# A two-layer convolution on one Trainium2 core: parameters loaded first, a shorter chain for the generated kernels, new queue orders for quads 2 and 3, new banks for the last pairs, one image normalised on GpSimd

## What is computed

```
x: (16, 32, 48, 48) float32
# L0: a (32, 32, 9, 9) kernel is generated from (sx, sy, angle) per channel pair
a = c*c*sx2 + s*s*sy2 ; b = c*s*(sx2 - sy2) ; d = s*s*sx2 + c*c*sy2 ; det = a*d - b*b
q = ia*xx*xx + 2*ib*xx*yy + id*yy*yy ; ker = exp(-0.5*q) ; ker /= sum(ker)
x = x + conv9x9(groupnorm(x, 16 groups), ker, zero padding) + bias
# L1: 5x5, reflect padding
x = x + conv5x5(groupnorm(x, 16 groups), weight)
```

## Time and profile before

| what | value |
|---|---|
| median of 3 runs | 280.61 us (280.49 to 281.2) |
| the profiled execution's own time | 280.59 us |
| its span, first to last instruction | 278.6 us |
| mean granted TensorE clock | 0.962 |
| busy PE | 228.2 us (82%) |
| busy DVE | 222.1 us (80%) |
| busy ACT | 156.9 us (56%) |
| busy POOL | 3.4 us (1%) |

### The profile page before, as it was taken

How to read it: one execution, slowest core, us unless ns; L and a number is a source line. 1 busy time by engine, 2 the same in 40 slices (tenths; PEclk the granted TensorE clock), 3 DMA queues, 4 the chain that set the end, 5 groups by cost and what they waited for, 6 DMA issues and landing times.

```text
span 278.6 us, 4041 instructions
## 1 busy us (share of the span) xinstructions
PE 228.2 (82%) x1388; PEld 138.3 (50%) x1388; DVE 222.1 (80%) x483; ACT 156.9 (56%) x320; POOL 3.4 (1%) x12
## 2 busy tenths in 40 slices
PE   0043766999799999997989999329999999996995
PEld 0042433566466566554646565115666665652552
DVE  1989999968999999999984999995168078987533
ACT  2966357998869757996629184407257002574310
POOL 1300000000000000000000000000000000000000
PEclk9998699999999999999999999859999999997999
DMA  7940001322004200035020000035200001522022
GB/s 256 358 178 0 0 0 46 85 65 65 0 0 118 69 0 2 1 90 177 5 85 2 0 0 4 1 104 166 87 0 0 2 0 30 154 88 85 2 85 85
DMA packets 7780, 17.37 MB, mean 62 GB/s; under 512 B 3280, under 2 KB 3920, under 8 KB 7760
## 3 DMA queue, kind: packets, MB, share of 16 engines
q1 hardware_dynamic: 6944, 16.78, 18.4%
q10 hardware_dynamic: 816, 0.33, 0.4%
HBM read 5.51 MB, written 4.72 MB: 37 GB/s over the span
## 4 chain that ended last, share of the span: by engine, by line
DVE 49%; PE 29%; ACT 10%; issue 9%; DMA 2%; DVEq 0%; ACTq 0%
PE banks L1253 17%; PE banks L1238 12%; DVE X L687 8%; DVE lo L654 6%; ACT P L974 3%; ACT junk L956 3%; DMA prm<-in_w 2%; DVE X L706 2%; DVE s L619 1%; DVE wl L513 1%; DVE arg L501 1%; DVE partU L609 1%; DVE partU L602 1%; ACT hi L997 1%; DVE wl L539 1%
## 5 line engine op out<-in xcount | busy, mean ns | idle before, releaser
L1238 PE MATMUL banks<-hi,wh 128*128 128x368 f16 (+4 forms) x288 | 51.8, 326 | 15.0 <-ACT wh L1029 6.2
L1238 PE MATMUL banks<-lo,wh 128*128 128x368 f16 (+4 forms) x288 | 50.4, 320 | 0.0
L1238 PE MATMUL banks<-hi,wl 128*128 128x368 f16 (+4 forms) x288 | 50.3, 320 | 0.0
L1238 PEld LDWEIGHTS banks<-hi,wh 128*128 128x128 f16 x288 | 27.9, 100 | 33.9 <-issue 10.9
L956 ACT ACTIVATE junk<-X 128x576 bf16<-128x576 f32 x60 | 41.0, 684 | 2.5 <-DVE X L687 0.5
L1253 PE MATMUL banks<-lo,wh 128*128 128x384 f16 x160 | 33.2, 340 | 8.4 <-DVE lo L654 8.4
L1238 PEld LDWEIGHTS banks<-lo,wh 128*128 128x128 f16 x288 | 28.2, 98 | 17.2 <-issue 0.2
L1238 PEld LDWEIGHTS banks<-hi,wl 128*128 128x128 f16 x288 | 28.1, 98 | 17.0
L1253 PE MATMUL banks<-hi,wh 128*128 128x384 f16 x160 | 32.1, 332 | 4.3 <-DVE X L712 2.8
L1253 PE MATMUL banks<-hi,wl 128*128 128x384 f16 x160 | 32.7, 336 | 0.0
L997 ACT CAST hi<-work 128x416 f16<-128x416 f32 x32 | 16.5, 539 | 20.8 <-DVE work L661 12.8
(11 more groups left out here) (127 smaller groups left out, 240.2 us busy)
## 6 DMA issues: line engine op xcount, KB each, us to landing
X<-in_x SPq DMA_DIRECT2D x8, 576.0 KB, 9.9
out<-X SPq DMA_DIRECT2D x7, 576.0 KB, 2.9
work<-X SPq DMA_DIRECT2D x8, 432.0 KB, 3.8
work<-X SPq DMA_DIRECT2D x8, 144.0 KB, 3.6
wh<-work SPq DMA_DIRECT2D x12, 72.0 KB, 2.1
wl<-work SPq DMA_DIRECT2D x12, 72.0 KB, 2.0
stage<-in_w SPq DMA_DIRECT2D x1, 640.0 KB, 7.1
work<-X SPq DMA_DIRECT2D x32, 12.0 KB, 2.3
```

The source lines that it names most:

```text
L1238: ins = nc.tensor.matmul(dst[:, :, o0:o1], wbuf[1][:, i, t * P:(t + 1) * P], src[:, :, o0 + dx:o1 + dx], start=(part == 0 and at == 0), st ...
```

## The change

- SyncE issues `prm` as its first load; the bias goes from SyncE to ScalarE, behind the tables.
- `covariance` and `exponent_parts` do several small products in one instruction each (`q` is numbered anew, and the squares 1, 4, 9, 16 come from the tables). GpSimd's two operations go to VectorE. The offsets are made by `offsets(1, 1)` and, behind the exponents of group 1, `offsets(2, 4)`. The exponentials wait for both, since they write over `centre`.
- The kernel sum takes one reduction over all taps (the outer taps counted twice) in place of one for each group.
- GpSimd normalises image 3 of quad 0; ScalarE the other three.
- `step(2)` and `step(3)` become `third_quad` and `fourth_quad`, with other orders on VectorE and ScalarE; `small_stats(1, 3)` and its square root stand earlier in the second quad. TensorE's order and SyncE's other orders stay.
- Pairs 6 and 7 get other banks than pairs 4 and 5.

```diff
-BANKS2 = ((6, 2, 3, 0), (1, 4, 5, 6))
+BANKS2 = ((6, 2, 3, 0), (1, 4, 5, 6)) * 3 + ((2, 3, 0, 1), (4, 5, 6, 2))
...
+            sp.dma_start(prm[:, :, :], w0).then_inc(prm_loaded, 16)
             load(0)
             load(1)
             sp.dma_start(stage[:, :, :], w1).then_inc(stage_loaded, 16)
-            sp.dma_start(bias_c[1][:, :], bias).then_inc(bias_loaded, 16)
...
             def covariance():
                 mul = ALU.mult
-                done(tt(wq[:, 0, :], prm[:, :, 0], prm[:, :, 0], mul))
-                done(tt(wq[:, 1, :], prm[:, :, 1], prm[:, :, 1], mul))
+                done(tt(wq[:, :, :], prm[:, :, 0:2].rearrange("p o a -> p a o"), prm[:, :, 0:2].rearrange("p o a -> p a o"), mul))
+                stage_end()
+                done(tt(q[:, 5, :], wq[:, 0, :], wq[:, 1, :], ALU.subtract))
...
                 stage_end()
-                done(tt(q[:, 1, :], scq[:, 1, :], wq[:, 0, :], mul))
-                done(tt(q[:, 2, :], scq[:, 0, :], wq[:, 1, :], mul))
-                done(tt(q[:, 3, :], scq[:, 0, :], wq[:, 0, :], mul))
-                done(tt(q[:, 4, :], scq[:, 1, :], wq[:, 1, :], mul))
-                done(tt(q[:, 5, :], wq[:, 0, :], wq[:, 1, :], ALU.subtract))
-                stage_end()
-                done(tt(q[:, 6, :], q[:, 1, :], q[:, 2, :], ALU.add))
-                done(tt(q[:, 7, :], q[:, 3, :], q[:, 4, :], ALU.add))
+                done(tt(q[:, 1:5, :].rearrange("p (a b) o -> p a b o", a=2), wq[:, :, :].unsqueeze(2).to_broadcast([P, 2, 2, C]),
+                        scq[:, :, :].unsqueeze(1).to_broadcast([P, 2, 2, C]), mul))
                 done(tt(q[:, 8, :], q[:, 0, :], q[:, 5, :], mul))
                 stage_end()
+                done(tt(q[:, 6:8, :], q[:, 2:0:-1, :], q[:, 3:5, :], ALU.add))
+                done(tt(q[:, 10, :], q[:, 8, :], q[:, 8, :], mul))
+                stage_end()
                 done(tt(q[:, 9, :], q[:, 6, :], q[:, 7, :], mul))
-                done(tt(q[:, 10, :], q[:, 8, :], q[:, 8, :], mul))
                 stage_end()
                 done(tt(q[:, 11, :], q[:, 9, :], q[:, 10, :], ALU.subtract))
                 stage_end()
                 done(nc.vector.reciprocal(q[:, 12, :], q[:, 11, :]))
                 stage_end()
-                done(stt(q[:, 13, :], q[:, 7, :], -0.5, q[:, 12, :], mul, mul))
-                done(tt(q[:, 14, :], q[:, 8, :], q[:, 12, :], mul))
-                done(stt(q[:, 15, :], q[:, 6, :], -0.5, q[:, 12, :], mul, mul))
-                stage_end()
-                MARK["quadratic"] = count[0]
+                done(stt(q[:, 13:15, :], q[:, 6:8, :], -0.5, q[:, 12, :].unsqueeze(1).to_broadcast([P, 2, C]), mul, mul))
+                done(tt(q[:, 15, :], q[:, 8, :], q[:, 12, :], mul))
+                stage_end()
...
                 dve.wait_ge(tab_loaded, 16)
-                done(tt(centre, per_row(yy2_t), per_chan(q[:, 15, :]), mul))
-                for k in range(1, 5):
-                    done(ts(ak[:, k - 1, :], q[:, 13, :], float(k * k), None, mul))
+                done(tt(centre, per_row(yy2_t), per_chan(q[:, 13, :]), mul))
+                done(tt(ak[:, :, :], squares_t.unsqueeze(2).to_broadcast([P, PAD1, C]),
+                        q[:, 14, :].unsqueeze(1).to_broadcast([P, PAD1, C]), mul))
                 stage_end()
                 done(tt(centre, centre, per_row(mask_t), ALU.add))
-                stage_end()
-                MARK["centre"] = count[0]
-                for k in (3, 2, 1):
-                    done(tt(ca_rows(k), centre, per_chan(ak[:, k - 1, :]), ALU.add))
-                    MARK["offset", k] = count[0]
+                done(tt(bt[:, :, :], per_row(yy_t), per_chan(q[:, 15, :]), mul))
+                stage_end()
+            def offsets(first, last):
+                n = last - first + 1
+                at = slice(first - 1, last)
+                done(tt(ca[:, at, :].rearrange("p k (e o) -> p k e o", o=C), centre.unsqueeze(1).to_broadcast([P, n, NE, C]),
+                        ak[:, at, :].unsqueeze(2).to_broadcast([P, n, NE, C]), ALU.add))
+                MARK["offsets"] = count[0]
+                stage_end()
             def exponents(g):
                 btf = bt[:, :, :].rearrange("p e o -> p (e o)")
                 for t in range(3 * g, 3 * g + 3):
                     k = t - PAD1
                     if k != 0:
-                        if abs(k) == PAD1:
-                            dve.wait_ge(exponents_pool, 2)
-                        else:
-                            dve.wait_ge(exponents_pool, 1)
-                            dve.wait_ge(dve_w, MARK["offset", abs(k)])
                         done(stt(arg[:, t, :], btf, float(k), ca[:, abs(k) - 1, :], ALU.mult, ALU.add))
                 MARK["exponents", g] = count[0]
...
                 done(tt(slot(1)[:, at, :], slot(2)[:, at, :], block1(1)[:, at, :], ALU.add))
                 MARK["blocks", g] = count[0]
-            def tap_sums(g):
-                dve.wait_ge(dve_w, MARK["blocks", g])
-                at = slice(3 * g, 3 * g + 3)
-                done(nc.vector.tensor_reduce(ksg[:, g, :], slot(1)[:, at, :].rearrange("p k (r o) -> p o (k r)", o=C), AX_X, ALU.add))
             def kernel_sum():
-                stage_end()
-                done(stt(ksum[:, :], ksg[:, 0, :], 2.0, ksg[:, 1, :], ALU.mult, ALU.add))
+                dve.wait_ge(dve_w, MARK["blocks", 0])
+                done(stt(twice, slot(1)[:, 0:3, :], 2.0, slot(1)[:, 3:6, :], ALU.mult, ALU.add))
+                stage_end()
+                done(nc.vector.tensor_reduce(ksum[:, :], twice.rearrange("p k (r o) -> p o (k r)", o=C), AX_X, ALU.add))
                 MARK["ksum"] = count[0]
             def kernel_reciprocal():
...
                 angles()
                 covariance()
                 exponent_parts()
+                offsets(1, 1)
                 exponents(1)
+                offsets(2, PAD1)
                 exponents(0)
                 first_stats()
                 exponents(2)
                 for at, g in enumerate((1, 0)):
                     block_sums(g, at)
-                    tap_sums(g)
                 kernel_sum()
                 outer_sum1(0)
...
-                ends1(2)
-                stream1(2, 0)
-                stream1(2, 7)
+                streams1_ends(2)
                 low_halves(1, 2, range(2, 4))
                 middle2(1)
                 rows2(1)
-                wide1(2)
-                for i in (3, 4, 5, 6):
-                    stream1(2, i)
+                small_stats(1, 3)
+                streams1_wide(2)
                 low_halves(1, 2, range(4, 8))
                 end2(1, 2)
                 end2(1, 3)
...
+            def third_quad():
+                small_stats(2, 1)
+                middle1(2, 0)
+                rows1(2, 0)
+                end1(2, 2)
+                end1(2, 3)
+                streams2(2)
+                low_halves(2, 2, range(4))
+                middle1(2, 1)
+                rows1(2, 1)
+                streams1_near(3)
+                low_halves(1, 3, range(2))
+                streams2(3)
+                middle1(2, 2)
+                rows1(2, 2)
+                low_halves(2, 3, range(2))
+                middle2(2)
+                rows2(2)
+                low_halves(2, 3, range(2, 4))
+                end2(2, 2)
+                end2(2, 3)
+            def fourth_quad():
+                streams1_ends(3)
+                low_halves(1, 3, range(2, 4))
+                middle2(3)
+                rows2(3)
+                streams1_wide(3)
+                low_halves(1, 3, range(4, 8))
+                end2(3, 2)
+                end2(3, 3)
+                small_stats(2, 2)
+                middle1(3, 0)
+                rows1(3, 0)
+                streams2(4)
+                low_halves(2, 4, range(4))
+                end1(3, 2)
+                end1(3, 3)
+                middle1(3, 1)
+                rows1(3, 1)
+                streams2(5)
+                middle1(3, 2)
+                rows1(3, 2)
...
         @block.scalar
         def _(act):
-            act.dma_start(prm[:, :, :], w0).then_inc(prm_loaded, 16)
...
             def kernel_exponentials(g):
-                act.wait_ge(exponents_pool, 2)
-                act.wait_ge(dve_w, MARK["exponents", g])
...
-            normalise1(0)
+            normalise1(0, range(QI - 1))
...
             channel_sums(2, 1, range(2))
             high_halves(1, 2, range(2, 4))
             channel_sums(2, 1, range(2, 4))
+            standard_deviation(1, 3)
             high_halves(1, 2, range(4, 8))
...
+            read_m1(2, 0)
+            normalise1(3, range(2))
+            standard_deviation(2, 1)
+            normalise2(2)
+            high_halves(2, 2, range(4))
+            normalise1(3, range(2, 4))
+            read_m1(2, 1)
+            normalise2(3)
+            high_halves(1, 3, range(2))
+            read_m1(2, 2)
+            read_m2(2)
```

(120 more changed lines are left out.)

12 lines of the change are left out of this document (5 added, 7 removed).

## The result

The changed kernel takes **257.77 us** (median of 4 runs, 257.58 to 258.15), the kernel before beside it 280.85: a ratio of 0.918 (95% interval 0.9163 to 0.9198). Forecast were 258.8, range 257.4 to 263.0: the measured time lies near the lower end of the range, and the two medians are 23.1 us apart where 21.8 were forecast. The profiled execution took 257.84 with a span of 256.1; TensorE's mean granted clock is 0.987 in place of 0.962, its busy share 87% (82%), VectorE's 86% (80%).

The account below looks back on a forecast made before the run. TensorE was taken as the bound, so its idle time and the slow clock behind it could be won: 3.7 + 13.6 + 4.5 = 21.8 off 280.6 gives 258.8 us, range 257.4 to 263.0.

Parts of the forecast that it names:

- The start: Up to the first sum of normalised rows: earlier parameters and a shorter VectorE chain save 3.7 us (ends 2.3 and 4.5).
- the 3.39 of the chain: At the start, tiny dependent operations from the moments to the last exponents: claimed to stay at 3.39 us.
- VectorE's shorter chain: VectorE between parameter landing and statistics: merged small operations end at 15.6 against 16.76, 1.15 us saved.
- GpSimd, 0.35 of VectorE's time: At the start, GpSimd normalising the last image slows VectorE beside it by 0 to 1.4 us; 0.35 taken.
- rival (b): Start gains only 0.7 of 3.7: parameters land no earlier or GpSimd contention holds VectorE up; 261.8 us, chance 0.12.
- Rival (d): Slower than before: the first sum of rows waits for GpSimd's image; 281.5 us or more, chance 0.02.
- Quads 2 and 3: Middle stage: new orders remove TensorE's idle time and the slow clock behind it, saving 13.6 us (ends 10.5 and 13.7).
- The replay: Quads 2 and 3's new queues stepped through in old times: pair 3's low half has 1.25 us to spare.
- Rival (a): VectorE becomes the bound in the middle, pair 3's low half 3 us later than forecast; 261.9 us, chance 0.12.
- The tail: Pairs 6 and 7: other banks remove the 2.76 us wait and slow clock, saving 4.5 us (ends 2.8 and 4.6).
- Rival (c): In the tail another release stands behind the bank, so the gap stays; 263.3 us, chance 0.04.
- the idle time between 35 and 129: Waits before instructions whose queue order stays: moved unchanged in the forecast, with 0.4 us allowed at the range's low end.

## Why the prediction was right

- **The start, 3.7.** The sum came out, in part by luck (below). The first sum of rows was put at 21.8 and came at 21.81, the moments at 13.25 and came at 13.30, the parameters at 2.8 and came at 2.83. The chain from landing to the tables' first use took 3.65, forecast 3.66 (9.31 less 5.65). The choice that carried it was to take the quiet copy's 2.0 for the parameters, and to ask what ends second: the run with the old loads (2.3, not 2.8) shows ScalarE's sums as that second bound. Three misses cancel behind the moments. 13.25 and the 3.39 of the chain are 16.64, the prediction went on with 16.5; the exponents came at 16.29, 2.99 behind the copy, since the 0.32 of idle time before them was not there; and GpSimd cost 0.22 more than was put. VectorE's shorter chain was put at 1.15 and is worth 1.0 where it is the bound.
- **GpSimd, 0.35 of VectorE's time.** Mis-sized: it was 0.57 (0.82 and 0.86 in place of 0.55, and 21.81 against 21.24 without the neighbour). My argument, one input read and so nearer to nothing, did not hold: the two-input additions of VectorE were stretched, as the Trainium skill's "GPSIMD Engine Reference" (key points) has it. The trace agrees for a part only: the three exponents at 16.29, with two inputs too, took their usual 1.49 beside GpSimd. So the sign that was named for rival (b), rows of 0.8 beside GpSimd, did show, while its time of 261.8 did not come: the stretch was 0.57, not the 3.0 that (b) needs. Rival (d) is out as well, the image took GpSimd 2.46. That the move itself saves nothing was right, ScalarE alone is done at 20.97; it was even a loss in the span, and the time outside took 0.3 of that back.
- **Quads 2 and 3, 13.6.** 13.8 by the timelines, 14.2 by the run with the old orders. The replay held for VectorE almost to the tenth: in its old times it had VectorE waiting for ScalarE's read until 157.35, which with the shift of 4.15 is 153.20, and it was 153.28. The 0.2 that the sum was short is that it took 142.09 for the end of TensorE's last matmul, where the starts give 141.93. Slack: 1.25 said, 1.0 found; TensorE came 0.18 earlier than in the replay and VectorE 0.05 later. Rival (a) did not come. Its price, 1.3 of slow clock for 1.8 of wait, no run tests; the wait of 3.40 cost 5.1 in all.
- **The tail, 4.5.** 4.6 by the timelines; putting the old banks back costs 4.6 by the time and 4.3 by the profile, putting the new ones in takes off 4.6 by the profile. Rival (c) is out, since no wait is left.
- **Missed, 1.0 in all** (258.8 against 257.84 in the profile), in small pieces of one sign. They bring the time to the 257.8 that the prediction gives for its three terms at their high ends; that 257.77 lies inside the range is owed to the 0.4 added for the idle time between 35 and 129. The pieces: 0.4 between 25 and 125 us, 0.3 in the two later stages, 0.25 outside the span (1.99 before, 1.74 now). Of the 0.4, 0.35 lies in one place. In the kernel before VectorE stood idle between two dependent operations,

```profile
85.88 0.96 DVE L647 SCALAR_TENSOR_TENSOR partA<-partA,partB 128x768 f32<-128x768 f32 x1 [0.47 <-DVE partU L644]
```

and in the changed kernel the same operation starts at 81.73, 0.1 behind the end of its predecessor. No edit touches these. The two variants of the kernel before (new loads, new banks) have the stretch from quad 1's first product to the statistics as it was, 22.1 us; the changed kernel and its variants, that with the old loads too, have 21.7. So it goes with the kernel, but not with the loads, banks or orders. What causes it was not tried. "The idle time that I move as it is" is the step that was too coarse here.

## What to carry to other kernels

Where each engine runs a queue in a fixed order, replay the new order by hand with the old rows' durations, and note for each hand-over when it is wanted and when it stands; the smallest difference is both the forecast's weak point and the slack that an experiment can measure. Two edits on one path need not add: ask which chain ends second (here loads 2.8 alone, 2.3 with the shorter chain). A bank that the last eviction of the stage before still holds costs its wait and, in two of three profiles here, a slow clock behind it: 2.8 and 1.4 to 1.7 us for one line of bank numbers. A small load that a chain waits for goes ahead of the large ones: 2.1 and 2.2 us to landing here, against 4.9 and 6.3.

## What was not expected of the hardware

- The granted clock behind a wait is not settled by its length. After 2.75 us of idle time ten matmuls ran slow in one profile, after 2.76 most of fifteen in another (the kernel before) and none in a third; after 3.40 us one part ran at full speed, then about three did not. Behind the wait of 8.43 or 8.44, which four profiles have, the slow matmuls cost 1.4, 1.9, 2.4 and 2.6 us; the kernel before's own, 1.4, is the least, so part of its spread, and of the 23.1 between the medians, may be this. The 2.22 us at about 40 us, followed by full speed in the profile of the changed kernel, was followed in its next one by nine matmuls of 2.87 us instead of 1.57, and by slow ones in seven of the fourteen profiles in all. There the time did not change, since the next product otherwise waits 1.36 us for its mirrored weights.
- GpSimd beside VectorE: 0.3 us more for each of two additions, nothing for the three exponents next to them.
- The time outside the span is not a constant: 1.74 to 1.84 us with the image on GpSimd, 2.07 to 2.15 without, 1.9 to 2.0 for the kernel before and its variants. It comes with the kernel, not with the run, so spans of different kernels should not be compared to better than 0.4 us.
